# Block 0 of x loaded as squares in halves and turned on VectorE, all of W1 folded first, norms and gate multiplied into x

## The chip, the cores and the metric

The kernel runs on one core of a Trainium2 chip. The metric is device time in microseconds (us) of one execution; before the change it is 106.59 us, the median of 3 runs (106.47 to 107.71).

## What is computed

x is (2, 1024, 256) in float32. Each token is rotated by quaternions (a left one from `cond_256`, a right one from `q_right`, each divided by its norm) and multiplied by a gate per lane, then goes through a feed-forward layer with one expert of eight, weighted by its router probability. (The reference runs the gate through an FFT along the tokens and back; since the gate does not depend on the token, that is a plain multiplication.)

```python
x_spectral = jnp.fft.fft(x_quat, axis=1)
x_filtered = jnp.fft.ifft(x_spectral * spectral_gate, axis=1).real
x_rotated = hamilton(q_left_n, hamilton(x_filtered, q_right_conj))
...
probs = softmax(xf @ Wr.T)
h = gelu(xf @ W1[7] + b1[7], approximate=False)
y = (h @ W2[7] + b2[7]) * probs[:, 7:8]
return x + y
```

## The kernel before

The rotation is linear, so the kernel never rotates x. It folds the rotation matrix R into W1 (256 x 1024) and into the router's weights, with matrix products in float32, and then multiplies x by the folded weights. The 2048 tokens go in 4 blocks b of 512. The hidden size 1024 is 8 tiles f of 128, and W1 is folded in 4 chunks of 256 columns (two tiles each). The 256 channels are KC = 2 halves k of 128.

For accuracy with fast products every operand is split into a high part, rounded to float32r, and a low part, the rest: hi·hi, hi·lo and lo·hi are added. So every folded chunk, every block of transposed x and every hidden tile needs a copy for its high part (mostly on ScalarE) and a subtraction for its low part (VectorE).

**Steady part.** `first_product(b, f)` on TensorE makes pre-activations in one of two PSUM banks `pre` (6 matmuls of 512 columns). `gelu(b, f)` on ScalarE reads them twice, for `h_hi` and for `h_all`; `low_hidden` on VectorE makes `h_lo`. `second_product(b, f)` follows two tiles later. `first_product(b, f)` waits until the `h_all` of tile f - 2 is read out of its bank: for b = 0, f = 2 it is `h_ready` 1.

**Opening, which the change is about.** Block 0 of x comes as two halves of 256 tokens, 2 KB to a partition, into `x_in`, and TensorE transposes them by an identity (L696) into two PSUM banks. R exists first as `R_raw`, without the norms and the gate, since these come later (`inv_norms` is a power on GpSimd). The first chunk of W1 is folded with `R_raw` (`first_fold`, L556), and VectorE multiplies `scale`, the norms and the gate, into it while it splits it (L389, L394). `scaled_rotation` (L372) makes R for the other three chunks. `opening()` makes tiles f = 0 and 1 of block 0 in halves of 256 tokens (L597, 24 matmuls). Then come the folds of chunks 1 to 3 (L568), and then `first_product(0, 2)` (L627). Blocks 1 to 3 come as 32 x 32 squares (`x_sq`, rows of 256 bytes), and VectorE turns them into `xT` (`turn_x`, L420).

Each engine runs its own list in the order in which it is written; semaphores order them against each other. All loads are issued from SP's queue, in the order small, first W1, x in two halves, rest of W1, W2 in four pieces, squares of block 1, b2. Before everything TensorE runs `WARM_UP` matmuls on zeros (L550). In the trace each float32 matmul is two instructions, each with its weight load, so 6 of them show as 12.

## Time and profile before

| | |
|---|---|
| median of 3 runs | 106.59 us (106.47 to 107.71) |
| profiled execution | 105.98 us |
| its span on the core | 104.2 us |
| TensorE (PE) busy | 100.1 us, 96% of the span |
| VectorE (DVE) busy | 66.5 us, 64% |
| ScalarE (ACT) busy | 48.9 us, 47% |
| first matmul of `first_product(0, 2)` | at 12.36 us |

PE is TensorE's matmuls and PEld its weight loads, which overlap them. POOL is GpSimd, SP the engine that issues the DMAs. A chain of work follows what ended last back to what released it.

### The profile page before, as it was taken

What the parts mean: (1) busy time and instruction counts of PE and PEld (TensorE: products, weight loads), DVE (VectorE), ACT (ScalarE), POOL (GpSimd) and SP (SyncE); (2) the same over time, 40 slices, a digit from 0 to 9 for tenths busy, and PEclk for the clock granted to TensorE, in tenths of its full rate; (3) what the DMA queues carried; (4) which work ended last, traced back from release to release, by engine and by line L of the source; (5) the groups of instructions that cost most, each with busy time, mean ns of one, the idle gap of its engine ahead of it and who ended that gap; (6) DMA issues with size and microseconds to landing.
All of it is one profiled execution on the core that took longest, in us unless ns stands there. A gap on an engine that the chain in (4) does not pass through costs nothing.

```text
span 104.2 us, 1505 instructions
## 1 busy us (share of the span) xinstructions
PE 100.1 (96%) x572; PEld 84.9 (82%) x572; DVE 66.5 (64%) x143; ACT 48.9 (47%) x79; POOL 25.7 (25%) x16
## 2 busy tenths in 40 slices
PE   7899999999999999999999999999999999999990
PEld 7679888878888888888888878788888878888980
DVE  1599589878264999288224997272494972378451
ACT  5046794444441484484424544834424544442700
POOL 3400000029999300000000000069998000000000
PEclk9999999999999999999999999999999999999998
DMA  1999910170004222350600050000006040000005
GB/s 25 287 388 369 178 26 6 42 159 0 0 0 123 88 101 101 74 127 0 200 2 3 0 208 0 0 0 0 0 0 201 6 201 0 0 0 0 0 5 196
DMA packets 9222, 8.12 MB, mean 78 GB/s; under 512 B 6784, under 2 KB 7424, under 8 KB 9216
## 3 DMA queue, kind: packets, MB, share of 16 engines
q1 hardware_dynamic: 8928, 7.78, 25.4%
q10 hardware_dynamic: 288, 0.26, 0.7%
q8 instruction: 4, 0.07, 0.3%
q14 instruction: 2, 0.02, 0.1%
HBM read 5.94 MB, written 2.10 MB: 77 GB/s over the span
## 4 chain that ended last, share of the span: by engine, by line
PE 91%; DMA 4%; SPq 1%; DVE 1%; DVEq 0%; issue 0%
PE pre L627 40%; PE acc L634 25%; PE acc L642 15%; DMA x_in<-in_x 4%; PE pre L597 3%; PE lT_bank L586 2%; PE acc L638 1%; PE acc L636 1%; DVE y L462 1%; PE extra L568 1%; PE acc L568 1%; PE lT_bank L568 1%; PE acc L696 1%; SPq L217 0%; SPq L214 0%; DVEq L69 0%
## 5 line engine op out<-in xcount | busy, mean ns | idle before, releaser
L304 ACT ACTIVATE h_hi<-pre,quats 128x512 fp32r<-128x512 f32 x32 | 22.1, 690 | 43.5 <-PE pre L627 42.5
L428 DVE TENSOR_TENSOR h_lo<-h_all,h_hi 128x512 fp32r<-128x512 f32 x32 | 21.8, 690 | 20.1 <-ACT h_all L308 19.8
L634 PE MATMUL acc<-w_parts,h_hi 128*128 128x512 f32 x116 | 32.3, 391 | 0.0
L634 PEld LDWEIGHTS acc<-w_parts,h_hi 128*128 128x128 f32 x116 | 21.5, 188 | 4.5
L627 PE MATMUL pre<-xT_hi,w_hi 128*128 128x512 f32 x60 | 24.0, 400 | 0.0
L627 PE MATMUL pre<-xT_lo,w_hi 128*128 128x512 f32 x60 | 23.7, 394 | 0.0
L642 PE MATMUL acc<-w_parts,h_lo 128*128 128x256 f32 x128 | 23.0, 283 | 0.0
L266 POOL TENSOR_TENSOR exps<-e_const,shifted 128x32 f32<-128x32 f32 x4 | 22.2, 5577 | 0.2
L642 PEld LDWEIGHTS acc<-w_parts,h_lo 128*128 128x128 f32 x128 | 20.0, 189 | 2.7 <-DVE h_lo L428 0.7
L308 ACT ACTIVATE h_all<-pre,quats 128x512 f32<-128x512 f32 x32 | 21.8, 683 | 0.0
L627 PE MATMUL pre<-xT_hi,w_lo 128*128 128x512 f32 x60 | 18.7, 392 | 0.0
L261 POOL TENSOR_TENSOR shifted<-logits_wide,logit_max 128x64 f32<-128x64 f32 x2 | 1.3, 672 | 52.0 <-DVE logit_max L435 52.0
L627 PEld LDWEIGHTS pre<-xT_hi,w_lo 128*128 128x128 f32 x60 | 11.3, 188 | 2.6
L627 PEld LDWEIGHTS pre<-xT_hi,w_hi 128*128 128x128 f32 x60 | 11.3, 188 | 2.1 <-issue 0.4
L627 PEld LDWEIGHTS pre<-xT_lo,w_hi 128*128 128x128 f32 x60 | 11.3, 189 | 1.6
L457 DVE SCALAR_TENSOR_TENSOR part<-acc,prob,rest 128x256 f32<-128x256 f32 x16 | 7.4, 477 | 5.8 <-PE acc L642 5.7
L462 DVE SCALAR_TENSOR_TENSOR y<-acc,prob,part 128x256 f32<-128x256 f32 x16 | 7.6, 483 | 1.5 <-PE acc L642 1.0
L452 DVE SCALAR_TENSOR_TENSOR rest<-b_all,prob,x_in 128x256 f32<-128x256 f32 x16 | 6.9, 481 | 0.1
L420 DVE STREAM_TRANSPOSE xT<-x_sq 128x512 f32<-128x512 f32 x6 | 6.1, 1090 | 0.0
L377 DVE TENSOR_TENSOR xT_lo<-xT,xT_hi 128x512 fp32r<-128x512 f32 x6 | 4.1, 717 | 0.0
L550 PE MATMUL lT_bank<-const-float32-0.0 128*128 128x128 f32 x12 | 2.9, 432 | 0.8 <-PEq L756 0.8
L277 ACT ACTIVATE xT_hi<-xT 128x512 fp32r<-128x512 f32 x6 | 3.4, 630 | 0.0
(68 smaller groups left out, 59.3 us busy)
## 6 DMA issues: line engine op xcount, KB each, us to landing
x_sq<-in_x SPq DMA_DIRECT2D x12, 128.0 KB, 3.6
x_in<-in_x SPq DMA_DIRECT2D x3, 512.0 KB, 3.4
out<-y SPq DMA_DIRECT2D x3, 512.0 KB, 2.6
w<-in_W SPq DMA_DIRECT2D x4, 256.0 KB, 6.3
w_rest<-in_W_rest SPq DMA_DIRECT2D x1, 768.0 KB, 5.8
x_in<-in_x SPq DMA_DIRECT2D x2, 256.0 KB, 3.9
w_first<-in_W_first SPq DMA_DIRECT2D x1, 264.0 KB, 2.7
out<-y SPq DMA_DIRECT2D x2, 128.0 KB, 1.7
```

The source lines that it names most:

```text
L266: nc.gpsimd.tensor_tensor(exps[i][:, :, :], e_const[:, :].unsqueeze(2).to_broadcast([P, TT, NE]), shifted[:, i * TT:(i + 1) * TT, :], ALU. ...
L304: nc.scalar.activation(h_hi[:, s, :], pre[f % 2][:, :], ACT.Gelu, bias=b1_cols[:, f:f + 1]).then_inc(h_hi_ready, 1)
L308: nc.scalar.activation(h_all[:, s, :], pre[f % 2][:, :], ACT.Gelu, bias=b1_cols[:, f:f + 1]).then_inc(h_ready, 1)
L377: nc.vector.tensor_tensor(xT_lo[b % 2][:, k, :], xT[b % 2][:, k, :], xT_hi[b % 2][:, k, :].bitcast(F32), ALU.subtract).then_inc(xT_lo_read ...
L420: nc.vector.transpose(xT[b % 2][:, k, :].rearrange("p (j t s) -> p j s t", j=TT, s=QUADS), x_sq[:, :, k::KC].rearrange("p (s j) c -> p j s ...
L428: nc.vector.tensor_tensor(h_lo[:, s, :], h_all[:, s, :], h_hi[:, s, :].bitcast(F32), ALU.subtract).then_inc(h_lo_ready, 1)
L452: nc.vector.scalar_tensor_tensor(out=rest[:, j, :], in0=b2_all[:, :], scalar=prob[:, j:j + 1], in1=x_in[:, j, :], op0=ALU.mult, op1=ALU.ad ...
L457: nc.vector.scalar_tensor_tensor(out=part[:, j, :], in0=acc_low[j], scalar=prob[:, j:j + 1], in1=rest[:, j, :], op0=ALU.mult, op1=ALU.add) ...
L462: nc.vector.scalar_tensor_tensor(out=y[:, j, :], in0=acc_high[j], scalar=prob[:, j:j + 1], in1=part[:, j, :], op0=ALU.mult, op1=ALU.add).t ...
L627: last = nc.tensor.matmul(bank[:, :], w[:, k, cols], part_of_x[:, k, :], start=(n == 0), stop=(n == len(steps) - 1))
L634: nc.tensor.matmul(acc[j][:, :], rows, w2_parts[:, f, :, :], start=(f == 0), stop=False)
L642: return nc.tensor.matmul(acc_high[j], h_lo[:, f % SLOTS, j * P:(j + 1) * P], w2_parts[:, f, 0, :], start=False, stop=(f == FT - 1 or (b = ...
```

## The change

1. **Loads.** The first chunk of W1 and its last one are issued from ScalarE's queue, the two in between from SP's (four transfers of 256 to 264 KB in place of 264 and 768 KB). Block 0 of x is no longer loaded early as rows: eight transfers of 64 KB bring it as squares, in two halves, the first 4 for half 0. W2, b2, then block 0 of `x_in` (512 KB, for the addition at the end) and the squares of block 1 follow; the last wait until block 0 has been turned.
2. **Turning.** TensorE's 8 transposes and ScalarE's two copies into `xT` go. VectorE turns each half with two stream transposes (`turn_first_x`). A half is now every quad's first or last two tokens, so `opening()` reads and writes patterns of 128 x 2 columns.
3. **Scale.** `scaled_rotation` and the scaling of the first chunk go. `scale` is multiplied into x in the splits of every block: ScalarE's copy gets it as its scale, VectorE's subtraction becomes a `scalar_tensor_tensor`. The router's weights are scaled as before, since the router reads the unscaled `xT`.
4. **Order.** TensorE folds all four chunks before `opening()`. ScalarE takes over the high part of the first chunk, and does chunks 1 to 3 between and beside the splits of x, ahead of the first Gelu.
5. **Warm-up.** 15 float32 matmuls of 64 columns in place of 6 of 128. Both load 128 columns of weights each time.

```diff
-    WARM_UP = 6
+    WARM_UP = 15
...
+        fold_banks = [None] + [bank[:, :].rearrange("p (k f) -> p k f", k=KC) for bank in (acc[3], lT_bank, extra)]
...
+        def half_of(columns, half):
+            rows = slice(half * QUADS // 2, (half + 1) * QUADS // 2)
+            return columns.rearrange("p (n s) -> p n s", s=QUADS)[:, :, rows]
...
         def _(sp):
             sp.dma_start(quats[:, :], small).then_inc(q_loaded, 16)
-            sp.dma_start(w1_first[:, :, :], W1_first).then_inc(w1_loaded[0], 16)
-            for i in range(2):
-                tiles = slice(i * TT // 2, (i + 1) * TT // 2)
-                sp.dma_start(x_in[:, tiles, :], x_blocks[0, :, tiles, :]).then_inc(first_x_loaded[i], 16)
-            sp.dma_start(w1_rest[:, :, :], W1_rest).then_inc(w1_loaded[1], 16)
+            for i in range(1, N_CHUNKS - 1):
+                sp.dma_start(w1_rest[:, i - 1, :, :], W1_rest[i - 1]).then_inc(w1_loaded[i], 16)
+            for half in range(2):
+                some = slice(half * 2 * TT, (half + 1) * 2 * TT)
+                for q in range(QUADS):
+                    sp.dma_start(x_sq[q * SQ:(q + 1) * SQ, some, :], x_squares[0, q, :, some, :]
...
             for i in range(FT // W2_TILES):
...
+            sp.dma_start(b2_all[:, :], b2.to_broadcast([P, C])).then_inc(b2_loaded, 16)
+            sp.dma_start(x_in[:, :, :], x_blocks[0]).then_inc(x_loaded, 16)
...
+            sp.wait_ge(x_turned, turned(0))
             load_squares(1)
-            sp.dma_start(b2_all[:, :], b2.to_broadcast([P, C])).then_inc(b2_loaded, 16)
...
+            act.dma_start(w1_first[:, :, :], W1_first).then_inc(w1_loaded[0], 16)
+            act.dma_start(w1_rest[:, N_CHUNKS - 2, :, :], W1_rest[N_CHUNKS - 2]).then_inc(w1_loaded[N_CHUNKS - 1], 16)
...
             def split_first_x(half):
-                act.wait_ge(first_x_turned, half + 1)
-                nc.scalar.activation(xT_hi[0][:, :, half * HALF:(half + 1) * HALF], xT_ps[half],
-                                     ACT.Copy).then_inc(xT_hi_ready, 1)
+                for k in range(KC):
+                    act.wait_ge(x_turned, KC * half + k + 1)
+                    nc.scalar.activation(half_of(xT_hi[0][:, k, :], half), half_of(xT[0][:, k, :], half), ACT.Copy,
+                                         scale=scale[:, k:k + 1]).then_inc(first_xT_hi_ready, 1)
...
+                act.wait_ge(folded, k + 1)
+                nc.scalar.activation(w1_hi[:, k, chunk(0)], first_fold_banks[k], ACT.Copy
+                                     ).then_inc(w1_first_hi_ready, 1)
...
-            for half in range(2):
-                split_first_x(half)
-            for half in range(2):
-                copy_first_x(half)
+            for k in range(KC):
+                first_w1_high(k)
+            split_w1(1)
+            act.wait_ge(scale_ready, 1)
+            split_first_x(0)
+            split_w1(2)
+            split_first_x(1)
+            split_w1(3)
             for b in range(N_BLOCKS):
...
+            def split_x(b, k):
+                dve.wait_ge(xT_hi_ready, KC * (b - 1) + k + 1)
+                nc.vector.scalar_tensor_tensor(
+                    out=xT_lo[b % 2][:, k, :], in0=xT[b % 2][:, k, :], scalar=scale[:, k:k + 1],
+                    in1=xT_hi[b % 2][:, k, :].bitcast(F32), op0=ALU.mult, op1=ALU.subtract).then_inc(xT_lo_ready, 1)
...
+                    dve.wait_ge(first_xT_hi_ready, KC * half + k + 1)
+                    nc.vector.scalar_tensor_tensor(
+                        out=half_of(xT_lo[0][:, k, :], half), in0=half_of(xT[0][:, k, :], half), scalar=scale[:, k:k + 1],
+                        in1=half_of(xT_hi[0][:, k, :], half).bitcast(F32), op0=ALU.mult,
+                        op1=ALU.subtract).then_inc(first_xT_lo_ready, 1)
...
+            def turn_first_x(half):
+                dve.wait_ge(first_sq_loaded[half], 16 * QUADS)
+                rows = slice(half * QUADS // 2, (half + 1) * QUADS // 2)
+                for k in range(KC):
+                    nc.vector.transpose(
+                        xT[0][:, k, :].rearrange("p (j t s) -> p j s t", j=TT, s=QUADS)[:, :, rows, :],
+                        x_sq[:, :, k::KC].rearrange("p (s j) c -> p j s c", j=TT)[:, :, rows, :]
+                        ).then_inc(x_turned, 1)
...
-                nc.vector.scalar_tensor_tensor(
-                    out=w1_lo[:, k, chunk(0)], in0=first_fold_banks[k], scalar=scale[:, k:k + 1],
-                    in1=w1_hi[:, k, chunk(0)].bitcast(F32), op0=ALU.mult,
-                    op1=ALU.subtract).then_inc(w1_first_lo_ready, 1)
+                nc.vector.tensor_tensor(w1_lo[:, k, chunk(0)], first_fold_banks[k],
+                                        w1_hi[:, k, chunk(0)].bitcast(F32), ALU.subtract).then_inc(w1_first_lo_ready, 1)
...
                     dve.wait_ge(b2_loaded, 16)
-                    dve.wait_ge(first_x_loaded[j * 2 // TT], 16)
-                else:
-                    dve.wait_ge(x_loaded, 16 * b)
+                dve.wait_ge(x_loaded, 16 * (b + 1))
...
             for k in range(KC):
-                first_w1_high(k)
-            for k in range(KC):
                 first_w1_low(k)
-            for half in range(2):
-                split_first_x(half)
-            scaled_rotation()
+            turn_first_x(0)
+            split_w1(1)
+            split_first_x(0)
+            turn_first_x(1)
+            split_first_x(1)
             dve.wait_ge(wr_padded, 1)
             for k in range(KC):
                 take_router(k)
             split_w2(0)
-            split_w1(1)
...
             zeros = nc.const_aps.tensor(0.0, [P, P], F32)
             for _ in range(WARM_UP):
-                nc.tensor.matmul(lT_bank[:, 0:P], zeros, zeros, start=True, stop=True)
+                nc.tensor.matmul(lT_bank[:, 0:P // 2], zeros, zeros[:, 0:P // 2], start=True, stop=True)
...
             def fold(i):
-                if i == 1:
-                    pe.wait_ge(w1_loaded[1], 16)
-                    pe.wait_ge(R_ready, KC)
-                elif i == 3:
-                    pe.wait_ge(xT_lo_ready, 2)
-                    pe.wait_ge(xT_copied, 2)
+                pe.wait_ge(w1_loaded[i], 16)
...
-                    tokens = slice(half * HALF, (half + 1) * HALF)
                     for k in range(KC):
-                        last = nc.tensor.matmul(pre[f][:, tokens], w[:, k, f * P:(f + 1) * P], part_of_x[0][:, k, tokens],
+                        last = nc.tensor.matmul(half_of(pre[f][:, :], half), w[:, k, f * P:(f + 1) * P],
+                                                half_of(part_of_x[0][:, k, :], half),
...
                 for half in range(2):
-                    pe.wait_ge(xT_hi_ready, half + 1)
+                    pe.wait_ge(first_xT_hi_ready, KC * (half + 1))
...
-                for f in range(2):
-                    for half in range(2):
-                        pe.wait_ge(xT_lo_ready, half + 1)
-                        last = products(w1_hi, xT_lo, half, f, ends=True)
-                    last.then_inc(pre_done, 1)
+                    pe.wait_ge(first_xT_lo_ready, KC * (half + 1))
+                    for f in range(2):
+                        last = products(w1_hi, xT_lo, half, f, ends=(half == 1))
+                        if half == 1:
+                            last.then_inc(pre_done, 1)
...
-            pe.wait_ge(R_raw_ready, 1)
+            pe.wait_ge(R_ready, 1)
             first_fold()
-            pe.wait_ge(ident_ready, 1)
-            channels = x_in[:, :, :].rearrange("p j (m k) -> p j k m", k=KC)
-            for half in range(2):
-                pe.wait_ge(first_x_loaded[half], 16)
-                for k in range(KC):
-                    for j in range(TT // 2):
-                        last = nc.tensor.transpose(xT_ps[half][:, k, j * P:(j + 1) * P],
-                                                   channels[:, half * TT // 2 + j, k], ident[:, :])
-                last.then_inc(first_x_turned, 1)
-            opening()
             for i in range(1, N_CHUNKS):
                 fold(i)
+            opening()
```

TensorE's list begins so, before and then with the change (`acc`, `lT_bank`, `extra` are PSUM banks, `w_first` and `w_rest` raw W1, `w_hi` and `w_lo` the parts of folded W1). Before:

```order
1 L550 MATMUL lT_bank<-const-float32-0.0 128x128 x6
2 L556 MATMUL acc<-w_first,R_raw 128x264 x2
3 L696 MATMUL acc<-ident,x_in 128x128 x8
4 L597 MATMUL pre<-xT_hi,w_hi 128x256 x4
5 L597 MATMUL pre<-xT_hi,w_lo 128x256 x4
6 L597 MATMUL pre<-xT_hi,w_hi 128x256 x4
7 L597 MATMUL pre<-xT_hi,w_lo 128x256 x4
8 L597 MATMUL pre<-xT_lo,w_hi 128x256 x8
9 L568 MATMUL lT_bank<-w_rest,R 128x256 x2
10 L568 MATMUL extra<-w_rest,R 128x256 x2
11 L568 MATMUL acc<-w_rest,R 128x256 x2
12 L627 MATMUL pre<-xT_hi,w_hi 128x512
```

With the change:

```order
1 L557 MATMUL lT_bank<-const-float32-0.0 128x64 x15
2 L563 MATMUL acc<-w_first,R 128x264 x2
3 L569 MATMUL acc<-w_rest,R 128x256 x2
4 L569 MATMUL lT_bank<-w_rest,R 128x256 x2
5 L569 MATMUL extra<-w_rest,R 128x256 x2
6 L596 MATMUL pre<-xT_hi,w_hi 128x128x2 x4
7 L596 MATMUL pre<-xT_hi,w_lo 128x128x2 x4
8 L596 MATMUL pre<-xT_lo,w_hi 128x128x2 x4
9 L596 MATMUL pre<-xT_hi,w_hi 128x128x2 x4
10 L596 MATMUL pre<-xT_hi,w_lo 128x128x2 x4
11 L596 MATMUL pre<-xT_lo,w_hi 128x128x2 x4
12 L627 MATMUL pre<-xT_hi,w_hi 128x512
```

The three folds of `w_rest` stood between `opening()` and L627 and now stand ahead of `opening()`; the transposes are gone, and the last products of half 0 no longer wait behind those of half 1.

VectorE's list from the scale on, before:

```order
13 L364 TENSOR_TENSOR scale<-inv_both,quats 128x2
14 L389 TENSOR_SCALAR w_hi<-acc,scale 128x256 x2
15 L394 SCALAR_TENSOR_TENSOR w_lo<-acc,scale,w_hi 128x256 x2
16 L383 TENSOR_TENSOR xT_lo<-acc,xT_hi 128x2x256 x2
17 L372 TENSOR_SCALAR R<-R_raw,scale 128x128 x2
18 L400 TENSOR_SCALAR wr_wide<-acc,scale 128x8 x2
19 L411 CAST w_parts<-w 128x2x256
```

With the change:

```order
13 L376 TENSOR_TENSOR scale<-inv_both,quats 128x2
14 L405 TENSOR_TENSOR w_lo<-acc,w_hi 128x256 x2
15 L398 STREAM_TRANSPOSE xT<-x_sq 128x4x2x32 x2
16 L414 TENSOR_TENSOR w_lo<-acc,w_hi 128x2x256
17 L389 SCALAR_TENSOR_TENSOR xT_lo<-xT,scale,xT_hi 128x128x2 x2
18 L398 STREAM_TRANSPOSE xT<-x_sq 128x4x2x32 x2
19 L389 SCALAR_TENSOR_TENSOR xT_lo<-xT,scale,xT_hi 128x128x2 x2
20 L409 TENSOR_SCALAR wr_wide<-acc,scale 128x8 x2
21 L420 CAST w_parts<-w 128x2x256
```

Turning half 0 stands behind both low parts of the first chunk, and turning half 1 behind the low parts of chunk 1 and of half 0.

## Rows read from the trace of the kernel before

**Rows 1.** The page, part 1: busy us (share of the span), instructions.

```profile
PE 100.1 (96%) x572; PEld 84.9 (82%) x572; DVE 66.5 (64%) x143; ACT 48.9 (47%) x79; POOL 25.7 (25%) x16
```

**Rows 2.** The chain that ended last, in order of time: start us, us, what.

```profile
2.12 4.17 DMA x_in<-in_x
...
7.07 3.01 PE pre L597 x24
...
10.95 0.86 PE extra L568 x4
...
12.68 1.40 PE pre L627 x6
```

**Rows 3.** A window: stretch, its length, busy us per engine, PEclk, DMA share, GB/s.

```profile
12.36:104.20 91.84, 89.11 (x514) 75.23 (x512) 58.94 (x116) 43.08 (x70) 23.59 (x6) 1.00 0.18 54
```

**Rows 4.** Timeline of the opening: start us, us, engine, line, operation, shapes.

```profile
0.77 2.90 PE L550 MATMUL lT_bank<-const-float32-0.0 128*128 128x128 f32 x12 [0.77 <-PEq L756]
...
4.06 1.37 PE L556 MATMUL acc<-w_first,R_raw 128*128 128x264 f32 x4 [0.39 <-DMA w_first<-in_W_first]
...
4.95 0.16 DVE L364 TENSOR_TENSOR scale<-inv_both,quats 128x2 f32<-128x2 f32 x1
...
10.79 1.03 PE L568 MATMUL extra<-w_rest,R 128*128 128x256 f32 x4
```

**Rows 5.** Weight loads and matmuls by line: duration ns min/median/max, first and last start.

```profile
L550 PEld LDWEIGHTS lT_bank<-const-float32-0.0 x12: 288/333/333, 0.7 to 3.0; 128*128 128x128 f32 x12
L550 PE MATMUL lT_bank<-const-float32-0.0 x12: 421/421/553, 0.8 to 3.3; 128*128 128x128 f32 x12
L568 PEld LDWEIGHTS extra<-w_rest,R x4: 190/190/190, 10.6 to 11.2; 128*128 128x128 f32 x4
L568 PE MATMUL extra<-w_rest,R x4: 379/379/379, 10.8 to 11.4; 128*128 128x256 f32 x4
L586 PEld LDWEIGHTS lT_bank<-xT,wr_wide x64: 106/110/110, 21.0 to 67.4; 128*32 128x32 f32 x64
L586 PE MATMUL lT_bank<-xT,wr_wide x64: 272/273/297, 21.0 to 67.5; 128*32 128x128 f32 x64
```

**Rows 6.** Groups by line and shape: busy us, mean ns of one, idle before.

```profile
L286 ACT ACTIVATE w_hi<-lT_bank 128x512 fp32r<-128x512 f32 x1 | 0.6, 597 | 0.7 <-PE lT_bank L568 0.7
L277 ACT ACTIVATE xT_hi<-xT 128x512 fp32r<-128x512 f32 x6 | 3.4, 630 | 0.0
L272 ACT ACTIVATE gelu_scratch<-warm 128x1 f32<-128x1 f32 x1 | 0.2, 203 | 0.0
L304 ACT ACTIVATE h_hi<-pre,quats 128x512 fp32r<-128x512 f32 x32 | 22.1, 690 | 43.5 <-PE pre L627 42.5 <-PE pre L597 0.6
L357 DVE TENSOR_TENSOR R_raw<-lane_eye,M 128x256 f32<-128x256 f32 x1 | 0.4, 427 | 0.0
L394 DVE SCALAR_TENSOR_TENSOR w_lo<-acc,scale,w_hi 128x256 fp32r<-128x256 f32 x2 | 0.9, 476 | 0.0
L383 DVE TENSOR_TENSOR xT_lo<-acc,xT_hi 128x512 fp32r<-128x512 f32 x2 | 1.4, 692 | 0.2 <-ACT xT_hi L281 0.2
L433 DVE STREAM_TRANSPOSE logits_wide<-lT_bank 128x256 f32<-128x256 f32 x2 | 0.9, 449 | 0.8 <-PE lT_bank L586 0.8
L420 DVE STREAM_TRANSPOSE xT<-x_sq 128x512 f32<-128x512 f32 x6 | 6.1, 1090 | 0.0
```

**Rows 7.** Timeline later: pairs of one kind back to back (start us, us).

```profile
16.78 2.04 DVE L420 STREAM_TRANSPOSE xT<-x_sq 128x512 f32<-128x512 f32 x2
...
20.84 1.15 ACT L277 ACTIVATE xT_hi<-xT 128x512 fp32r<-128x512 f32 x2
```

**Rows 8.** Windows of the first loads, columns as in the window above.

```profile
0.00:5.90 5.90, 4.68 (x19) 3.96 (x20) 2.73 (x16) 1.49 (x2) 2.15 (x10) 1.00 0.62 185
7.00:10.00 3.00, 3.00 (x26) 3.00 (x26) 2.79 (x8) 2.04 (x4) 0.00 (x0) 1.00 1.04 387
10.00:13.00 3.00, 3.00 (x16) 2.56 (x15) 1.62 (x4) 2.28 (x5) 0.00 (x0) 1.00 1.35 190
```

More of the change, by code:

```diff
@@ L42, in adaln_ffn @@
     NE = W1_first.shape[2] - CHUNK
-    F = CHUNK + W1_rest.shape[2]
+    F = CHUNK * (1 + W1_rest.shape[0])
     LANES = C // 4
@@ L142, in adaln_ffn @@
         logitsT = lT_bank[:, 0:2 * P].rearrange("p (j t) -> p j t", j=2 * TT)
-        HALF = BLOCK // 2
-        xT_ps = [bank[:, :].rearrange("p (k t) -> p k t", k=KC) for bank in acc[2:]]
         first_fold_banks = [bank[:, 0:CHUNK] for bank in acc[:KC]]
         wr_ps = [bank[:, CHUNK:CHUNK + NE] for bank in acc[:KC]]
-        fold_banks = [None] + [bank[:, :].rearrange("p (k f) -> p k f", k=KC) for bank in (lT_bank, extra, acc[3])]
+        fold_banks = [None] + [bank[:, :].rearrange("p (k f) -> p k f", k=KC) for bank in (acc[3], lT_bank, extra)]
         q_loaded = sem("q_loaded")
-        first_x_loaded = [sem(f"first_x_loaded{i}") for i in range(2)]
-        w1_loaded = [sem(f"w1_loaded{i}") for i in range(2)]
+        first_sq_loaded = [sem(f"first_sq_loaded{i}") for i in range(2)]
+        w1_loaded = [sem(f"w1_loaded{i}") for i in range(N_CHUNKS)]
         w2_loaded = [sem(f"w2_loaded{i}") for i in range(FT // W2_TILES)]
@@ L182, in adaln_ffn @@
         xT_lo_ready = sem("xT_lo_ready")
+        first_xT_hi_ready = sem("first_xT_hi_ready")
+        first_xT_lo_ready = sem("first_xT_lo_ready")
         logitsT_done = sem("logitsT_done")
@@ L317, in _ @@
                     gelu(b, f)
-                    if b == 0 and f == 0:
-                        split_w1(2)
-                        split_w1(3)
                     if f == 4 and b < LAST:
@@ L380, in split_first_x @@
-            def split_first_x(half):
-                tokens = slice(half * HALF, (half + 1) * HALF)
-                dve.wait_ge(xT_hi_ready, half + 1)
-                nc.vector.tensor_tensor(xT_lo[0][:, :, tokens], xT_ps[half], xT_hi[0][:, :, tokens].bitcast(F32),
-                                        ALU.subtract).then_inc(xT_lo_ready, 1)
-            def first_w1_high(k):
-                dve.wait_ge(folded, k + 1)
-                nc.vector.tensor_scalar(w1_hi[:, k, chunk(0)], first_fold_banks[k], scale[:, k:k + 1], None,
-                                        ALU.mult).then_inc(w1_first_hi_ready, 1)
+            def split_x(b, k):
[3 more added lines that the diff above has]
+                    in1=xT_hi[b % 2][:, k, :].bitcast(F32), op0=ALU.mult, op1=ALU.subtract).then_inc(xT_lo_ready, 1)
@@ new lines, in split_first_x @@
+            def split_first_x(half):
+                for k in range(KC):
+                    dve.wait_ge(first_xT_hi_ready, KC * half + k + 1)
[11 more added lines that the diff above has]
+                        ).then_inc(x_turned, 1)
@@ L555, in first_fold @@
                 for k in range(KC):
[L556 removed]
+                    nc.tensor.matmul(acc[k][:, 0:CHUNK + NE], R[:, 4 * k:4 * k + 4, :], w1_first[:, k, :],
                                      start=True, stop=True).then_inc(folded, 1)
             def fold(i):
[L560 to L566 removed]
+                pe.wait_ge(w1_loaded[i], 16)
                 for k in range(KC):
[L568 removed]
+                    nc.tensor.matmul(fold_banks[i][:, k, :], R[:, 4 * k:4 * k + 4, :], w1_rest[:, i - 1, k, :],
                                      start=True, stop=True).then_inc(folded, 1)
@@ L750 @@
         "W1_first": np.concatenate([W1[:, :, :2 * P], router], axis=2),
-        "W1_rest": W1[:, :, 2 * P:],
+        "W1_rest": W1[:, :, 2 * P:].reshape(P, 2, -1, 2 * P).transpose(2, 0, 1, 3),
         "W2": W2,
```

48 lines of the change are left out of this document (15 added, 33 removed).

## Prediction

> **What bounds the kernel now.** The page's shares come first: TensorE is busy for 100.1 of 104.2 us [rows 1]. The chain that ended last says where it is not waited for: it starts with the load of x (until 6.3 us), and from 7.07 us on it is TensorE's work without a gap, `opening()`, the three folds, and at 12.68 us the products of tile 2 [rows 2]. So the kernel is TensorE's list behind a start-up. I cut it where `first_product(0, 2)` starts, at 12.36 us: the stretch behind it, 91.84 us, holds 514 of 572 matmuls [rows 1, 3], and the change leaves every one of them as it is. The question is only at which time that instruction starts with the change.
>
> Before, TensorE hides a latency there: `opening()` ends at about 10.1 us, and while ScalarE makes the two Gelus that free the first `pre` bank, TensorE does the three folds of 0.86 us [rows 2]. With the folds ahead of `opening()`, nothing stands between `opening()` and `first_product(0, 2)`; both Gelus of tile 0, 0.69 us each [rows 6], are then waited for.
>
> **The change, part by part.**
>
> *Warm-up.* The first fold starts at 4.06 us, 0.4 us after the warm-up's end, when R and the first W1 are there [rows 4]. The warm-up's 12 instructions took 2.90 us, the last one 0.42 [rows 4, 5]: (2.90 - 0.42) / 11 = 0.225 us from start to start, and about 0.213 without the first, longer one. Now there are 30. Do 64 columns in place of 128 make one shorter? Only if the matmul sets the pace and not its weight load of 128 columns, which stays. At this stage a weight load took 288 to 333 ns, later 190 ns, and one of 32 columns 110 ns [rows 5]. So 96 columns cost 80 ns later on, 128 cost 107, and at the start 98 ns more than that, some 205 ns. I take it that the load sets the pace, at 0.213 us each, while the clock is at its lower level. The matmul rows show the levels: 128 columns in 0.213 us at the start, 256 columns in (1.03 - 0.38) / 3 = 0.217 us at 10.8 us [rows 4, 5], which is half of the 2.4 GHz and all of it (the column PEclk reads 1.00 for the start too [rows 8], so it doesn't show this). The rise falls into the first fold, whose four took 1.37 us and not 4 x 0.22 [rows 4], so at about 4.5 us, after work without a gap over 0.4 us since 0.77 us. Until 4.55 us some 18 of the 30 have started (one at 0.77, the next at 1.12, then every 0.213), and the other 12 at a faster load's 0.12 us (my value; 107 ns is the bound from below) take 1.45 us more: **the first fold starts at 6.05 us, 2.0 us later than now.**
>
> The Trainium skill, TensorE: Matmul & The Clock Gate, section LDWEIGHTS, gives a load as its columns divided by 1.2, in ns, so 107 ns for 128 columns, with no slower level. By it the 30 instructions would take 0.77 + 30 x 0.107 = 4.0 us, and the warm-up would end when R is ready. The rows of this case contradict it for the start-up; a run with the new shape decides.
>
> *Folds.* 16 instructions of 0.22 us, 4 for each chunk. From 6.05: the halves k of chunk 0 are complete at 6.65 and 7.10 (a result comes 0.16 after its issue slot), chunk 1 at 7.96, all four at 9.68.
>
> *ScalarE.* Its copy costs 0.60 us for 512 columns out of PSUM, 0.63 out of SBUF, and 0.20 for one column [rows 6]: 0.40 and 0.42 for 256, and 0.11 less when the next follows directly (two took 1.15 [rows 7]). High parts of chunk 0: 7.10 and 7.54. Chunk 1: 8.0 to 8.6.
>
> *VectorE*, in the order of its list. Free since the scale, 5.11 [rows 4], it waits for ScalarE: low parts of chunk 0 (0.43 each, as 256 columns of `R_raw` [rows 6]) end at 8.01. Turning half 0: no row has this shape. 512 columns cost 1.09, two in a row 2.04, and 256 columns of another pattern 0.45 [rows 6, 7]; I take 0.63, nearer to the same pattern with a fixed part, so k = 0 at 8.56, k = 1 at 9.03, and 0.45 is the bound from below. ScalarE's high parts of half 0: 9.02 and 9.49. VectorE's low part of chunk 1 (0.69) until 9.56, low parts of half 0 (0.476 each, as L394 [rows 6]) until 9.96 and 10.35, turning half 1 until 10.89 and 11.36, ScalarE's high parts at 11.35 and 11.82, low parts at 11.87 and 12.34.
>
> *opening().* Its 24 matmuls took 3.01 us, 0.125 each [rows 2]. Half 0 is done long before. Half 1: 8 matmuls from 11.86 to 12.86, then two for tile 0, which is complete at 12.86 + 0.25 + 0.17 = 13.28 us.
>
> *Gelu.* The first of the two starts at 13.32, and the second ends 0.69 - 0.11 + 0.69 later, 14.59 (the overlap as above). `first_product(0, 2)` starts at 14.66 us, against 12.36: **2.3 us later.**
>
> *Loads.* 1.09 MB (33 + 264 + 786 KB) go ahead of the squares; the trace had moved 185 GB/s x 5.9 us = 1.09 MB by 5.9 us [rows 8]. A backlog of rows of 256 bytes went at 190 GB/s, one of longer rows at 387 [rows 8]. 262 KB take 1.4 us: half 0 is there at about 7.3, half 1 at 8.7, each with 0.4 us of doubt. Neither is waited for: VectorE comes to them at 7.9 and 10.3. The squares of block 1 are now issued behind the last turn, at about 11.4 us, and are needed by the turn that now starts at 16.78 [rows 7], so at some 19: hidden.
>
> *Scale in x, later blocks.* Six subtractions of 0.72 us become `scalar_tensor_tensor`, perhaps 0.1 longer, on an engine that is busy for 64% [rows 1]; copies with a scale stay on ScalarE (47%). Both are covered by TensorE. The removed transposes and copies stood on TensorE and ScalarE ahead of 7.07 us, where the load was waited for; on the new chain they count nothing.
>
> *Sum.* 2.3 us on top of the profiled 105.98 or the median of 106.59 (the profiled one is 0.6 lower; the outer 1.8 us beside the span stay). I forecast **106.59 + 2.3 = 108.9 us**.
>
> **Rivals.**
>
> 1. *The warm-up is no longer than before* (a 64-column instruction takes 0.107 us). Then the folds run from 4.1, and x sets the time: VectorE turns half 0 from 7.0, and the same steps put `first_product(0, 2)` at 13.7, +1.4 us: **108.0 us**; with x there at 6.2, +0.6. The weight-load rows speak against it, what the skill's page states for it.
> 2. *The clock rises later*, since TensorE streams only 64 columns in each 0.213 us, half as much as in the trace. All 30 then run slowly, until 7.3 us, and some of the folds too, at 0.43 in place of 0.22: +1.25, and up to +0.9 for the first folds that stand on the chain. **110.3 us**, from +3.5 on. The rise at 4.5 us behind denser work [rows 4] leaves this open.
> 3. *The patterns of two adjacent columns are slow* in `opening()` and in the splits: 0.25 in place of 0.125 us per matmul adds 1.9 us, **110.8 us**. The router's matmuls read every fourth column and take no longer for it (273 ns [rows 5]); ScalarE's and VectorE's have no such row.
> 4. *Not slower.* If the warm-up ends at 4.1, half 0 is there at 6.2, a turn costs the 0.45 us of the other transpose [rows 6], and the small copies come out 0.1 lower, `first_product(0, 2)` starts at 12.2: **106.4 us**. This one is decided by the turns: at 0.63 it is +0.6 instead.
>
> **How the numbers follow.** The forecast 0.50, with 108.1 to 109.8 of its own (turns at 0.45: +1.7; dearer small splits: +2.85; the clock's rise 0.5 us earlier or later: 0.2 either way). Rival 1 0.25, rival 2 0.12, rival 3 0.07, rival 4 0.06. The range from 107.4 to 110.6 us leaves out rival 4, the lower end of rival 1 and half of rivals 2 and 3. 2% is 2.1 us, about what a measurement here can tell from no change, and it cuts the forecast's own case: 0.33 of the 0.50 lie above 108.7. With rivals 2 and 3 slower is 0.52; same is 0.17 + 0.25 + 0.04 = 0.46; faster 0.02.
>
> **What would show it.** The first fold at about 6.05 us behind a warm-up that ends without a gap; against it a warm-up that ends at 4. VectorE idle from 5.1 to 7.1 us and then busy without a wait until 12.3. A gap on TensorE between the end of `opening()` and `first_product(0, 2)` of about 1.2 us, with the releaser ScalarE's `h_all`. The start of that instruction at 14.7 us, and 91.8 us behind it. A stretch behind it that is not 91.8 us would make the prediction wrong altogether.

## The result

The changed kernel takes 112.23 us (median of 4 runs, 112.2 to 112.91) against 106.53 us (4 runs, 105.54 to 107.71): ratio 1.058, 95% interval 1.050 to 1.067. Slower was forecast, but with 108.9 us and a range up to 110.6 us. The cost is about two and a half times the forecast one. Some executions are over 1.5% longer than the fastest of their kernel; the ratios leave them out and compare with executions of the kernel before from the same session, the medians hold them all.

| | before | changed | forecast |
|---|---|---|---|
| median | 106.53 | 112.23 | 108.9 |
| span of the profiled execution | 104.2 | 110.4 | 106.5 |
| first fold starts | 4.06 | 7.20 | 6.05 |
| opening() starts | 6.99 | 11.91 | 9.5 |
| tile 0 of block 0 complete | 9.6 | 17.2 | 13.3 |
| first_product(0, 2) starts | 12.36 | 18.64 | 14.66 |

The page of the changed kernel, part 1, for [rows 1]:

```profile
PE 105.8 (96%) x582; PEld 90.2 (82%) x582; DVE 67.7 (61%) x145; ACT 49.8 (45%) x81; POOL 25.9 (23%) x16
```

The windows ahead of and behind `first_product(0, 2)` (stretch, length, busy us of PE, PEld, DVE, ACT, POOL, PEclk, DMA share, GB/s), for [rows 3]:

```profile
0.00:18.64 18.64, 16.88 (x70) 15.05 (x71) 8.54 (x30) 7.07 (x14) 2.15 (x10) 1.00 0.78 206
18.64:110.40 91.76, 88.97 (x512) 75.17 (x512) 59.13 (x116) 42.70 (x68) 23.72 (x6) 1.00 0.16 52
```

So the cut was the right one: 91.76 us lie behind it, 91.84 before. All of the loss, 18.64 - 12.36 = 6.28 us, is ahead of it. The chain in order of time (start us, us, what), for [rows 2]:

```profile
0.77 6.64 PE lT_bank L557 x30
7.41 1.87 PE acc L563 x4
9.27 1.00 PE acc L569 x4
10.28 0.86 PE lT_bank L569 x4
11.14 0.86 PE extra L569 x4
12.01 5.20 PE pre L596 x22
...
17.23 0.69 ACT h_hi L316
17.92 0.59 ACT h_all L318
```

It was forecast that x and VectorE's list would bind from 7.9 us on. Instead TensorE binds from its first instruction to 17.2 us, and three parts of it are longer than forecast: the warm-up, the first fold (1.87 us for four, at about half the rate of the 0.86 that four cost later), and `opening()`, 5.2 us in place of 3.0. (ScalarE's high parts of half 0, late by the same slow folds, end at 11.77 us and the last fold's slot at 11.84, so both let `opening()` start at 11.91.) The warm-up's group in the page's part 5 (busy us, mean ns of one, idle before), for [rows 5]:

```profile
L557 PE MATMUL lT_bank<-const-float32-0.0 128*128 128x64 f32 x30 | 6.6, 422 | 0.8 <-PEq L746 0.8
```

The products of `opening()` with `w_lo`, by their line (duration ns min/median/max, first and last start us), before and then with the change:

```profile
L597 PE MATMUL pre<-xT_hi,w_lo x8: 280/282/283, 7.5 to 8.8; 128*128 128x256 f32 x8
```

```profile
L596 PEld LDWEIGHTS pre<-xT_hi,w_lo x8: 207/208/209, 12.6 to 16.1; 128*128 128x128 f32 x8
L596 PE MATMUL pre<-xT_hi,w_lo x8: 405/409/417, 12.9 to 16.3; 128*128 128x256 f32 x8
```

The 30 warm-up instructions end at 7.41 us: (6.64 - 0.42) / 29 = 0.2145 us each, to the last one, although each streams only 64 columns. The matmuls of `opening()` are 24 in 5.56 us from 11.91 to 17.47, 0.23 each in place of 0.125, at a time when the folds just ahead of them run at full clock (0.216 us for 256 float32 columns, in the rows of 0.86 for four).

### The profile page after: what moved, and what is told of

The parts are those of the page before. It is cut to its first block, busy times and chain, and to the rows that moved or that the text cites. A ratio compares the mean times of both kernels' runs of the same rounds, so it can differ in the third digit from the quotient of the medians.

```text
span 110.4 us, 1535 instructions
## 1 busy us (share of the span) xinstructions
PE 105.8 (96%) x582; PEld 90.2 (82%) x582; DVE 67.7 (61%) x145; ACT 49.8 (45%) x81; POOL 25.9 (23%) x16
## 4 chain that ended last, share of the span: by engine, by line
PE 95%; ACT 1%; DVE 1%; DVEq 0%; issue 0%
PE pre L627 38%; PE acc L634 24%; PE acc L642 14%; PE lT_bank L557 6%; PE pre L596 5%; PE lT_bank L586 2%; PE acc L563 2%; PE acc L638 1%; PE acc L636 1%; PE acc L569 1%; DVE y L470 1%; PE extra L569 1%; PE lT_bank L569 1%; ACT h_hi L316 1%; ACT h_all L318 1%; DVEq L69 0%
## 5 line engine op out<-in xcount | busy, mean ns | idle before, releaser
L627 PE MATMUL pre<-xT_hi,w_hi 128*128 128x512 f32 x60 | 23.9, 398 | 1.0 <-ACT h_all L318 1.0
L627 PE MATMUL pre<-xT_lo,w_hi 128*128 128x512 f32 x60 | 23.7, 394 | 0.0
L627 PE MATMUL pre<-xT_hi,w_lo 128*128 128x512 f32 x60 | 18.7, 392 | 0.0
L627 PEld LDWEIGHTS pre<-xT_hi,w_hi 128*128 128x128 f32 x60 | 11.3, 188 | 3.4 <-issue 1.8
L627 PEld LDWEIGHTS pre<-xT_hi,w_lo 128*128 128x128 f32 x60 | 11.3, 188 | 2.6
L627 PEld LDWEIGHTS pre<-xT_lo,w_hi 128*128 128x128 f32 x60 | 11.3, 189 | 1.6
L557 PE MATMUL lT_bank<-const-float32-0.0 128*128 128x64 f32 x30 | 6.6, 422 | 0.8 <-PEq L746 0.8
L557 PEld LDWEIGHTS lT_bank<-const-float32-0.0 128*128 128x128 f32 x30 | 6.5, 332 | 0.7 <-issue 0.7
L382 DVE SCALAR_TENSOR_TENSOR xT_lo<-xT,scale,xT_hi 128x512 fp32r<-128x512 f32 x6 | 4.3, 761 | 0.0
```

Source lines behind the costliest of these rows:

```text
L557: nc.tensor.matmul(lT_bank[:, 0:P // 2], zeros, zeros[:, 0:P // 2], start=True, stop=True)
L627: last = nc.tensor.matmul(bank[:, :], w[:, k, cols], part_of_x[:, k, :], start=(n == 0), stop=(n == len(steps) - 1))
```

## Experiments

All times of the tile-2 products are starts of the first matmul of `first_product(0, 2)` in the profiled execution. ("Short loads" are warm-up matmuls with weights of 64 columns.)

| kernel | tile-2 products, us | time, us | ratio (95%) |
|---|---|---|---|
| before | 12.36 | 106.53 | |
| changed | 18.64 | 112.23 | 1.058 (1.050 to 1.067) |
| changed, old warm-up | 16.30 | 110.15 | 1.037 (1.029 to 1.045) |
| before, new warm-up | 16.30 | 110.14 | 1.035 (1.026 to 1.044) |
| changed, 15 warm-up matmuls of 128 columns | 16.28 | 109.81, one run | |
| changed, warm-up with short loads | 16.08 | 109.66, one run | |
| changed, x packed for reading | 17.2 | 110.72, one run | |
| changed, PSUM written packed | 18.8 | 112.29, one run | |
| changed, both repairs | 14.48 | 108.0 | 1.0155 (1.009 to 1.022) |
| both repairs, folds behind `opening()` | 15.54 | 109.47 | 1.0275 (1.018 to 1.037) |
| both repairs, reordered | 13.26 | 106.95 | 1.0064 (1.003 to 1.009) |
| reordered, warm-up with short loads | 15.63 (the slowest of 12) | 107.05 | 1.003 (0.999 to 1.007) |
| before, x from ScalarE's queue | 16.11 (the slowest of 6) | 108.53 | 1.013 (1.002 to 1.023) |
| before, warm-up with short loads | 13.62 | 106.6 | 0.997 (0.992 to 1.002) |

### The warm-up, out of the changed kernel and into the old one

```diff
-    WARM_UP = 15
+    WARM_UP = 6
...
-                nc.tensor.matmul(lT_bank[:, 0:P // 2], zeros, zeros[:, 0:P // 2], start=True, stop=True)
+                nc.tensor.matmul(lT_bank[:, 0:P], zeros, zeros, start=True, stop=True)
```

> The changed kernel with the old warm-up, 6 float32 matmuls of 128 columns in place of 15 of 64. Theory (the long warm-up and the late rise of the clock cost about 4 us, the two-column patterns in opening() the rest): the warm-up ends at 3.7 us, the first fold starts at 4.1, the folds of chunks 1 to 3 take 0.86 us each, the tile-2 products start at about 14.5 us in place of 18.6, time about 108.3 us (ratio 1.02). Rival (the warm-up is hidden, x and the new VectorE chain set the time): no change, 112.2 us.

> The kernel before, with only the new warm-up (15 matmuls of 64 columns). Theory (weight loads set the pace at 0.213 us, and the clock stays low while 64 columns are streamed): the warm-up ends at about 7.2 us, the first fold runs at 0.44 us a matmul and the clock rises at about 8 to 9.5 us; tile-2 products 3.5 to 4.5 us later, time 110.3 to 111 us (ratio 1.035 to 1.045). Rival (the warm-up costs only because the other parts are on the new chain): under 1 us, ratio below 1.01.

The second came out as expected. The start of its chain:

```profile
0.77 6.63 PE lT_bank L550 x30
7.41 1.87 PE acc L556 x4
9.27 0.87 PE acc L696 x4
...
10.91 3.11 PE pre L597 x24
```

The new warm-up alone costs the old kernel 3.94 us of its start (16.30 against 12.36) and 3.5% in all. Taking it out of the changed kernel gives back 2.34 us of start (2.1 us in the median), less than the 4 expected. The chain of that run shows why the rest did not come back:

```profile
3.58 4.15 DMA x_sq<-in_x
...
7.75 0.66 DVE xT L398
...
8.50 0.95 ACT xT_hi L294 x2
...
9.58 5.28 PE pre L596 x22
```

With the warm-up gone, x binds (half 0 lands at 7.73 us, at the edge of the prediction's own 7.3 with 0.4 of doubt; the expectation of this run had left this wait out), and then the 5.3 us of `opening()`.

### What of the warm-up is slow

Weight loads of 64 columns, and 128 streamed columns, each in place of the new form:

```diff
-                nc.tensor.matmul(lT_bank[:, 0:P // 2], zeros, zeros[:, 0:P // 2], start=True, stop=True)
+                nc.tensor.matmul(lT_bank[0:P // 2, 0:P // 2], zeros[:, 0:P // 2], zeros[:, 0:P // 2], start=True, stop=True)
```

> The changed kernel with 15 warm-up matmuls of 64 columns whose weights are 64 columns too. If the weight load sets the pace: 0.107 us each in place of 0.213, the warm-up ends at 4.1 us, 3 us earlier. If something else does (a fixed cost per instruction): 0.213 stays and it ends at 7.2 us.

> The changed kernel with 15 warm-up matmuls of 128 columns in place of 64, same weight loads. Both theories give 0.213 us each while the clock is low. If the clock rises by what is streamed and not by how long TensorE has been issuing, it rises between 4.5 and 7 us inside the warm-up, which then ends at 6.1 to 7 us, with the folds at full clock from the first: tile-2 products at 16.3 to 17.3 us, about 110 to 111 us. Rival (the rise comes late whenever the warm-up is long): the warm-up ends at 7.2 us and the clock rises at 9 to 10 us again, 112.2 us.

The line of the warm-up with short loads, then with 128 streamed columns (columns as above):

```profile
L557 PEld LDWEIGHTS lT_bank<-const-float32-0.0 x30: 178/227/227, 0.7 to 3.8; 128*64 128x64 f32 x30
L557 PE MATMUL lT_bank<-const-float32-0.0 x30: 314/314/337, 0.8 to 3.9; 128*64 128x64 f32 x30
```

```profile
L557 PEld LDWEIGHTS lT_bank<-const-float32-0.0 x30: 190/333/334, 0.7 to 5.7; 128*128 128x128 f32 x30
L557 PE MATMUL lT_bank<-const-float32-0.0 x30: 273/421/552, 0.8 to 5.8; 128*128 128x128 f32 x30
L563 PE MATMUL acc<-w_first,R x4: 386/386/387, 5.9 to 6.6; 128*128 128x264 f32 x4
```

Half the columns to load, half the time: the last of 30 starts at 3.9 us in place of 7.0, 3.12 / 29 = 0.107 us each. Twice the columns to stream change nothing while the clock is low: 0.213 us each again. So the weight load set the pace at the lower clock, as the prediction had it from [rows 5]. By the Trainium skill, TensorE: Matmul & The Clock Gate, section LDWEIGHTS, 128 columns would load in 107 ns; here that is the load of 64 columns at the lower clock, and the measurement decides.

With 128 streamed columns the same 30 instructions let the first fold start at 5.9 us, 1.3 us earlier, and at full clock (386 ns, against 647 in the changed kernel). So the clock rose inside the warm-up, as forecast for the new form. With 64 it did not rise before about 9.4 us in any of the four runs with that form (the changed kernel, its two packed variants, and the kernel before with the new warm-up, at about 10). With 64 columns and short loads it rose in the first fold, from 4.1 us (of its four, the slowest took 666 ns and the median 386). So the number of matmuls did not decide. In all four runs whose warm-up joins a full load to a short stream the clock stayed low to 9.4 us or beyond, although TensorE had no gap, and this fits rival 2. The form is the likely cause and not a shown one: the wide form was run once, and the last section has a run with the old warm-up in which the clock was still low at 8 us.

### The two-column patterns, by side

> The changed kernel, with the high and low parts of block 0 of x packed by halves, so that opening() reads 256 adjacent columns and only writes the pattern of 128 x 2 into PSUM; the later tiles of block 0 write their 512 columns in the order 2 x 128 x 2. If the pattern costs on the reading side: 0.12 us per matmul in opening() in place of 0.23, tile-2 products at about 17.2 us, time about 110.8 us. If it costs on the writing side: 0.23 stays, and the later tiles of block 0 (36 matmuls) may double too, up to 8 us more.

> The changed kernel, with opening() writing 256 adjacent columns of PSUM and still reading patterns of 128 x 2. (Tokens of tiles 0 and 1 of block 0 come out in another order; the work is the same.) If the pattern costs on the writing side: 0.12 us per matmul in opening(), time about 110.8 us. If on the reading side: 0.23 stays, 112.2 us.

```diff
+        def packed(columns, half):
+            h = BLOCK // 2
+            return columns[:, half * h:(half + 1) * h].rearrange("p (n s) -> p n s", s=QUADS // 2)
...
-                    nc.scalar.activation(half_of(xT_hi[0][:, k, :], half), half_of(xT[0][:, k, :], half), ACT.Copy,
+                    nc.scalar.activation(packed(xT_hi[0][:, k, :], half), half_of(xT[0][:, k, :], half), ACT.Copy,
...
-                        out=half_of(xT_lo[0][:, k, :], half), in0=half_of(xT[0][:, k, :], half), scalar=scale[:, k:k + 1],
-                        in1=half_of(xT_hi[0][:, k, :], half).bitcast(F32), op0=ALU.mult,
+                        out=packed(xT_lo[0][:, k, :], half), in0=half_of(xT[0][:, k, :], half), scalar=scale[:, k:k + 1],
+                        in1=packed(xT_hi[0][:, k, :], half).bitcast(F32), op0=ALU.mult,
...
-                                                half_of(part_of_x[0][:, k, :], half),
+                                                part_of_x[0][:, k, half * BLOCK // 2:(half + 1) * BLOCK // 2],
...
+                into = bank[:, :]
+                if b == 0:
+                    into = into.rearrange("p (n h s) -> p h n s", h=2, s=QUADS // 2)
...
-                    last = nc.tensor.matmul(bank[:, :], w[:, k, cols], part_of_x[:, k, :],
+                    last = nc.tensor.matmul(into, w[:, k, cols], part_of_x[:, k, :],
```

The second run is the changed kernel with one edit:

```diff
-                        last = nc.tensor.matmul(half_of(pre[f][:, :], half), w[:, k, f * P:(f + 1) * P],
+                        last = nc.tensor.matmul(pre[f][:, half * BLOCK // 2:(half + 1) * BLOCK // 2], w[:, k, f * P:(f + 1) * P],
```

It leaves out putting the tokens of tiles 0 and 1 back in their order, so its output is not the right one, and it serves for times alone. `opening()` with packed reading, and with packed writing only:

```profile
L600 PE MATMUL pre<-xT_hi,w_lo x8: 280/283/283, 12.6 to 15.2; 128*128 128x256 f32 x8
```

```profile
L596 PE MATMUL pre<-xT_hi,w_lo x8: 405/409/417, 13.1 to 16.5; 128*128 128x256 f32 x8
```

With packed reading a matmul takes what it took before the change (283 and 282 ns in the median), with packed writing alone what it took with it (409 ns). So the whole cost lies in how the moving operand is read, and writing the pattern of 128 x 2 into PSUM costs nothing. Nor does the order 2 x 128 x 2 of the later tiles: six matmuls of tile 3 of block 0 take 1.39 us in the first of the two runs, and 1.39 in the kernel before.

### Both repairs

> The changed kernel with both repairs: old warm-up (6 of 128 columns) and x packed by halves for opening(). If the two costs add and nothing else is lost but the new chain through x and VectorE: the second half's high parts at 11.7 us as in the run with the old warm-up alone, tile-2 products at 14.6 us, 108.5 us, ratio 1.02, the forecast's mechanism without warm-up and patterns. Rival (more is lost elsewhere): over 109.5 us. Rival (x is not the bound): below 107.5 us.

The tile-2 products start at 14.48 us and the kernel takes 108.0 us: as expected, 14.6 and 108.5. The two repairs give back 2.34 and 1.46 us alone and 4.16 together. Their chain is the one that was forecast (x, VectorE's list, half 1's high parts, 10 matmuls, two Gelus):

```profile
3.58 3.93 DMA x_sq<-in_x
...
7.53 1.09 DVE xT L402 x2
8.62 0.52 DVE w_lo L418
9.14 0.77 DVE xT_lo L393 x2
9.91 0.58 DVE xT L402
...
10.52 1.01 ACT xT_hi L298 x2
...
11.57 1.48 PE pre L600 x10
```

So of the 6.28 us, 4.16 are the warm-up and the pattern, and 2.12 are what the other parts of the change cost together.

### The remaining two microseconds

> As the run with both repairs (ratio 1.0155, tile-2 products at 14.5 us), with the folds of the last two chunks behind opening() and their high parts behind the first two Gelus, as in the kernel before; loads and VectorE's list are not touched. Forecast's reading (the uncovered Gelus of tile 0 cost over a microsecond): tile-2 products at 13.3 us, ratio 1.005. Rival (TensorE sits idle ahead of opening() anyway, so the folds only change places with that idle time): 14.4 to 14.8 us, ratio unchanged.

> As the run with both repairs, and: the squares of x are issued on SP's queue ahead of the last two chunks of W1 (the second chunk goes with the first on ScalarE's), VectorE turns each half as soon as it is there, and the folds of the last two chunks stand behind opening() again, where they cover the Gelus of tile 0. Theory (x's arrival and VectorE's list set the time): half 0 lands at about 5.8 us in place of 7.7, tile-2 products at 12.0 to 12.8 us, 106.3 to 107 us, ratio 0.995 to 1.005. Rival (the clock's rise sets it): 13.5 us and more, ratio over 1.01.

```diff
-            for i in range(1, N_CHUNKS - 1):
-                sp.dma_start(w1_rest[:, i - 1, :, :], W1_rest[i - 1]).then_inc(w1_loaded[i], 16)
             for half in range(2):
...
+            for i in range(2, N_CHUNKS):
+                sp.dma_start(w1_rest[:, i - 1, :, :], W1_rest[i - 1]).then_inc(w1_loaded[i], 16)
...
-            act.dma_start(w1_rest[:, N_CHUNKS - 2, :, :], W1_rest[N_CHUNKS - 2]).then_inc(w1_loaded[N_CHUNKS - 1], 16)
+            act.dma_start(w1_rest[:, 0, :, :], W1_rest[0]).then_inc(w1_loaded[1], 16)
...
-            split_w1(1)
...
             split_first_x(0)
-            split_w1(2)
+            split_w1(1)
             split_first_x(1)
-            split_w1(3)
...
+                    if b == 0 and f == 0:
+                        split_w1(2)
+                        split_w1(3)
...
+            turn_first_x(0)
             for k in range(KC):
                 first_w1_low(k)
-            turn_first_x(0)
-            split_w1(1)
-            split_first_x(0)
             turn_first_x(1)
+            split_first_x(0)
             split_first_x(1)
+            split_w1(1)
...
-            for i in range(1, N_CHUNKS):
-                fold(i)
+            fold(1)
             opening()
+            for i in range(2, N_CHUNKS):
+                fold(i)
```

Moving the folds alone (the last piece of this diff, with `split_w1(2)` and `split_w1(3)` behind the Gelus of tile 0) missed both expectations: 109.47 us, ratio 1.0275 (1.018 to 1.037), tile-2 products at 15.54 us. Its windows (columns as above):

```profile
4.00:8.00 4.00, 3.73 (x8) 2.53 (x8) 1.29 (x5) 0.77 (x2) 0.78 (x1) 1.00 1.25 285
8.00:9.70 1.70, 0.08 (x2) 0.04 (x1) 1.70 (x4) 1.44 (x3) 0.00 (x0) 1.00 1.03 305
9.70:14.20 4.50, 4.50 (x25) 4.50 (x26) 3.84 (x10) 1.24 (x3) 0.00 (x0) 1.00 0.90 303
```

TensorE sat idle for 1.6 us ahead of `opening()`, and then ran at half speed: its first products took 415 ns and the last 280, with packed reading. (PEclk reads 1.00 there; the durations are what shows it.) The folds that stood in that gap before went behind it. What 14.4 to 14.8 us left out is this clock. That the cover of the Gelus is worth nothing is an estimate and not shown by this run: with both repairs the Gelus of tile 0 held the tile-2 products for 1.41 us (13.07 to 14.48), and the two folds put behind `opening()` take 2 x 0.86 = 1.72 us themselves.

The reordered kernel, with x's loads ahead of the last two chunks of W1 and the copies of VectorE and ScalarE in order of arrival besides, comes to 13.26 us and 106.95 us, ratio 1.0064 (1.003 to 1.009). Half 0 landed at 6.25 us, later than the 5.8 expected, and the tile-2 products started 0.46 us behind the end of the 12.0 to 12.8 given; the ratio too is just over the 0.995 to 1.005 expected. VectorE was busy without a wait from 6.35 to 10.4 us, so x and its list set the time, as that theory had it. Of the forms of the change that I ran it is the best, together with the one below that has another warm-up, and still not better than the kernel before.

### Two tries to beat both

> The kernel before, with the two halves of block 0 of x issued from ScalarE's queue ahead of its table load, at about 0.8 and 1.2 us in place of 1.64 and 2.1; nothing else. If the issue time delays x: both halves land 0.5 to 0.7 us earlier (5.3 and 6.3 before), opening() starts at 6.5 us in place of 7.0, 0.3 to 0.5 us less in all, ratio 0.996. If the loads share one bandwidth in any case, and the first W1 now comes later: ratio 0.999 to 1.003.

```diff
-            for i in range(2):
-                tiles = slice(i * TT // 2, (i + 1) * TT // 2)
-                sp.dma_start(x_in[:, tiles, :], x_blocks[0, :, tiles, :]).then_inc(first_x_loaded[i], 16)
...
         def _(act):
+            for i in range(2):
+                tiles = slice(i * TT // 2, (i + 1) * TT // 2)
+                act.dma_start(x_in[:, tiles, :], x_blocks[0, :, tiles, :]).then_inc(first_x_loaded[i], 16)
             act.wait_ge(warm_zeroed, 1)
```

A miss in the other direction: 108.53 us, ratio 1.013 (1.002 to 1.023), which rests on two of its six executions (106.76 and 108.27 us). The profiled one is the slowest, 109.74 us, so it shows how time is lost and not how much on the whole. Its loads (KB each, median us from issue to landing), and the first fold in its chain:

```profile
x_in<-in_x ACTq DMA_DIRECT2D x2, 256.0 KB, 4.0
w_first<-in_W_first SPq DMA_DIRECT2D x1, 264.0 KB, 4.6
quats<-in_small SPq DMA_DIRECT2D x1, 33.0 KB, 2.9
```

```profile
5.93 2.10 PE acc L556 x4
```

The first W1 took 4.6 us and the quaternions 2.9, against 2.7 and 1.9 in the kernel before. What x gained by its place was lost by the two transfers that everything waits for first: the fold started at 5.93 us, and at half speed behind 2.3 us of idle time. That the transfers of the two queues share one bandwidth is the likely reading; one slow execution does not show it.

> The kernel before, with a warm-up of 15 matmuls of 64 columns whose weights are 64 columns too (0.107 us each, so it ends at 4.0 us and not at 3.7, and leaves no idle time ahead of the first fold at 4.06). Theory (idle time of TensorE around 4 us lets the clock rise later in some executions, and the spread of the kernel before, 105.8 to 107.8 us, comes from that): the clock rises at 4.5 us, median 0.3 to 0.7 us lower with a smaller spread, ratio 0.994 to 0.998. Rival (the spread comes from elsewhere, or half as wide streaming makes the rise later): ratio 1.000 or above.

> The reordered kernel (ratio 1.0064) with the same short-load warm-up. Its opening is set by the arrival of x at 6.3 us and VectorE's list, so the clock's rise matters only for the folds ahead of it. Theory: tile-2 products at 13.3 to 13.6 us as before, ratio 1.003 to 1.008. Rival (a gap of 1.6 us on TensorE ahead of opening() together with narrower warm-up matmuls lets the clock rise late): 109 us and more.

```diff
-    WARM_UP = 6
+    WARM_UP = 15
...
-                nc.tensor.matmul(lT_bank[:, 0:P], zeros, zeros, start=True, stop=True)
+                nc.tensor.matmul(lT_bank[0:P // 2, 0:P // 2], zeros[:, 0:P // 2], zeros[:, 0:P // 2], start=True, stop=True)
```

The diff is against the kernel before; the reordered kernel gets the same line. In the kernel before: 106.6 us, ratio 0.997 (0.992 to 1.002), with a spread as wide as before (105.6 to 109.0). The ratio cannot be told from 1, and the idea that the idle time at 4 us makes the spread fell. In that profile (107.25 us) the second half of x landed at 7.69 us, against 6.29 in the profile of the kernel before (105.98 us):

```profile
2.12 5.57 DMA x_in<-in_x
```

The loads of the two kernels are the same, and so is their order. The tile-2 products start 1.26 us later (13.62 against 12.36), and the whole takes 1.27 us longer. So in this pair of executions the landing of x is enough to make the difference; what makes it land late is open. In the reordered kernel: 107.05 us, ratio 1.003 (0.999 to 1.007), as expected. Its profile can't say where the tile-2 products start on the whole: it is of the one execution that took 109.29 us. There TensorE sat idle for 1.77 us ahead of `opening()`, and the granted clock went back to the lower level inside it, which comes close to the rival:

```profile
10.30:13.80 3.50, 3.12 (x15) 3.05 (x15) 3.08 (x9) 0.32 (x1) 0.00 (x0) 0.51 1.01 281
```

No kernel here beats the one before beyond its interval.

## Why the prediction was wrong

- **The cut and the part behind it: right.** 91.76 us against 91.84; scaling x in later blocks is covered. The copy with a scale costs 0.72 us in place of 0.63 and the subtraction 0.76 in place of 0.72 (means), on engines that wait.
- **The weight load sets the warm-up's pace: right.** 0.2145 us each measured, 0.213 forecast, shown by the short loads. The working was weaker than its result: it took the shortest load of the start, 288 ns; with the median of 333 ns the same sum gives 0.25 us and not 0.205.
- **"The rise falls into the first fold, so at about 4.5 us", and the other 12 at 0.12: the step that failed first.** It took the moment of the rise from a warm-up that streamed 128 columns and gave it to one that streams 64. The form with 128 columns did behave so: its first fold started at about 5.9 us, 6.05 forecast. With 64 all 30 ran at 0.2145, and the first five fold instructions at or near half speed. What the runs show in its place is a rise at 9.4 us or later in all four runs of the new form; that the shorter stream is what delays it is likely, not shown. The folds' last slot ended at 11.84 us in place of 9.52: 7.20 - 6.05 = 1.15 us from the warm-up, 1.17 from the folds.
- **"Its 24 matmuls took 3.01 us, 0.125 each": the step that failed second.** The instruction has another access pattern than the row it was priced by. Read as two adjacent columns of every four, 256 columns take 0.23 us. The row that was to speak against it, the router's, is a float32 matmul, and a float32 instruction takes 0.217 us for 256 columns anyway [rows 4], where a float32r one takes 0.12. At that pace a slow read of 0.23 us would hardly show, so the row was weak evidence (no run tests the router's pattern in float32r).
- **Their meeting.** Rivals 2 and 3 were priced apart, 110.3 and 110.8 us, with chances of 0.12 and 0.07, as if one excluded the other. What both priced came true, and together they made a third case that no line of the range held: TensorE bound from its first instruction to the end of `opening()`. From the folds' end at 11.84 us, 5.6 us of `opening()`, then the two Gelus: 18.6.
- **x, VectorE's list, the Gelus: right in size, but not on the path.** With both repairs the list binds as described: half 0 lands at 7.5 (7.3 forecast), a half turn costs 0.64 us (0.63), the Gelus 1.28 and the step to the products 0.14 (1.27 and 0.07). ScalarE's high part of a half costs 0.52 there and 0.54 in the changed kernel, where 0.42 was taken; the scale adds to it, as in the later blocks. Rival 1, priced at +1.4 us, is what the repaired kernel is: +2.1 us of start, with x half a microsecond later than there and the dearer copies.
- **Not slower (rival 4) and faster: right to be small.** Even with both repairs and x moved ahead the two best forms are at 1.006 and 1.003.

## What to carry to other kernels

- Price a matmul by a row with the same operand type and the same access pattern on the moving side, not only the same number of columns. Where a half is a strided choice of columns, pack it when it is written; the copy that writes it is there anyway, and neither of the two orders tried on the PSUM side cost anything.
- A row of one warm-up does not tell when the clock rises under another form of it: run the form, and more than once. At the lower clock, shortening the streamed part from 128 to 64 columns while the load of 128 stays saved nothing: 0.213 us each either way.
- When two rivals hit the same engine in a row, price them together. A second DMA queue is not free for the first transfers: with x on ScalarE's, the first W1 came 1.9 us later and the quaternions 1.0 in the execution that was profiled.

## What the runs showed of the hardware

A float32r matmul that reads two adjacent columns of every four takes 0.227 to 0.23 us for 256 columns whatever the clock. In the run with short weight loads the clock fell for a stretch in the middle of `opening()`, and the matmuls did not slow down (same line in both stretches; windows, columns as above, and the weight loads of the line over both):

```profile
9.40:11.30 1.90, 1.90 (x9) 1.74 (x10) 1.76 (x5) 1.08 (x3) 0.00 (x0) 1.00 0.94 319
11.40:14.60 3.20, 3.20 (x16) 3.20 (x15) 1.95 (x6) 0.60 (x2) 0.00 (x0) 0.50 1.03 252
```

```profile
L596 PEld LDWEIGHTS pre<-xT_lo,w_hi x8: 209/309/312, 11.0 to 14.5; 128*128 128x128 f32 x8
```

The weight loads, 207 to 209 ns ahead of the fall, take 309 behind it; the matmuls take 405 to 417 and 407 to 412.

About 0.23 us is also what 256 columns cost at the lower clock (0.213). A slow read can thus look like a low clock in a profile, and what tells them apart is the weight loads, or a neighbour with a plain pattern: in the changed kernel the folds beside it, 256 float32 columns in 0.216 us.

When the clock rises was not settled. With the same warm-up of 6 matmuls of 128 columns the first fold of four took 1.37 us in the kernel before, 2.10 with the old warm-up in the changed kernel, and 1.16 with both repairs:

```profile
4.00 1.16 PE L567 MATMUL acc<-w_first,R 128*128 128x264 f32 x4 [0.32 <-DVE R L373]
```

TensorE had done the same in all three until 4 us. In the run with the folds behind `opening()`, again with that warm-up, the clock was still low when the second chunk ended at 8.1 us, behind no gap of over 0.6 us; four fold instructions took, from the start us,

```profile
4.27 2.10 PE acc L568 x4
6.37 1.72 PE acc L574 x4
```

against 0.86 to 0.89 at full clock. With short loads, too, it differs: in the changed kernel the clock rose in the first fold, in the kernel before not until its end (644 ns each, busy us and mean ns):

```profile
L556 PE MATMUL acc<-w_first,R_raw 128*128 128x264 f32 x4 | 2.0, 644 | 0.0
```

So the moment of the rise in one profile is in part a draw, worth about a microsecond or more, and not a property of the kernel alone. The new form's late rise stands out from it by being late four times of four.
